# A layer loop in another order, two PSUM banks to an instruction, and the stores issued by ScalarE

## The reference, cut to what matters

```python
x_ft = jnp.fft.rfft2(v)
out1 = jnp.einsum('bixy,ioxy->boxy', x_ft[:, :, :M1, :M2], W1)
out2 = jnp.einsum('bixy,ioxy->boxy', x_ft[:, :, -M1:, :M2], W2)
...
x1 = jnp.fft.irfft2(out_ft, s=(Sx, Sy))
x2 = jnp.einsum('bcxy,cd->bdxy', v, w_w[i]) + w_b[i][None, :, None, None]
v = x1 + x2
mean = jnp.mean(v, axis=(0, 2, 3), keepdims=True)
var = jnp.var(v, axis=(0, 2, 3), keepdims=True)
v = (v - mean) * jax.lax.rsqrt(var + BN_EPS)
v = v * bn_g[i][None, :, None, None] + bn_b[i][None, :, None, None]
if i < L - 1:
    v = jax.nn.relu(v)
```

## Time and profile before

| | |
|---|---|
| median of 3 runs | 3470.16 us (3431.05 to 3483.62) |
| the profiled execution | 3436.51 us, its span 3434.7 us |
| busy share of the span: TensorE, VectorE, ScalarE, GpSimd | 82%, 62%, 45%, 18% |
| mean granted clock of TensorE | 0.896 of full |
| evictions L794 in the three loops | 768, the first at 222.1, the last at 2015.6 us |
| data moved | 541 MB, 158 GB/s over the span |

### The profile page before, as it was taken

How to read it: one execution, slowest core, us unless ns; L and a number is a source line. 1 busy time by engine, 2 the same in 40 slices (tenths; PEclk the granted TensorE clock), 3 DMA queues, 4 the chain that set the end, 5 groups by cost and what they waited for, 6 DMA issues and landing times. The chain is left out here.

```text
span 3434.7 us, 105530 instructions
## 1 busy us (share of the span) xinstructions
PE 2801.5 (82%) x45316; PEld 1467.6 (43%) x45316; DVE 2131.9 (62%) x3133; ACT 1547.3 (45%) x3432; POOL 605.7 (18%) x758
## 2 busy tenths in 40 slices
PE   0389999997899999789999985833478862999999
PEld 0145555554455555345555542211266650333333
DVE  2677777676577777567777753016467654455555
ACT  1255666564566666456666642001101110566665
POOL 0002333110033321003332110000144430000000
PEclk9889999898899999889999997976777766999999
DMA  5036666553888887478888863971122202567775
GB/s 161 11 86 161 149 140 142 123 140 101 246 256 255 250 251 241 126 195 259 256 255 251 255 194 142 405 230 37 46 63 67 66 20 58 96 119 120 119 121 90
DMA packets 244004, 541.34 MB, mean 158 GB/s; under 512 B 77857, under 2 KB 124705, under 8 KB 229953
## 3 DMA queue, kind: packets, MB, share of 16 engines
q1 hardware_dynamic: 234320, 529.04, 56.5%
q10 hardware_dynamic: 9264, 6.11, 0.9%
HBM read 320.28 MB, written 214.78 MB: 156 GB/s over the span
## 5 line engine op out<-in xcount | busy, mean ns | idle before, releaser
L794 ACT ACTIVATE p_v<-p_ps,k_scale_bias 128x512 f32<-128x512 f32 x768 | 536.8, 777 | 533.8 <-PE p_ps L900 533.8
L778 POOL COPY k_xm<-p_sp 64x288 f32<-64x288 f32 x384 | 264.6, 689 | 1566.2 <-DVE p_sp L301 1549.4
L801 ACT ACTIVATE p_ps<-p_ps 128x512 f32<-128x512 f32 x768 | 454.7, 593 | 116.6 <-PE p_ps L915 116.6
L900 PEld LDWEIGHTS p_ps<-k_idfty,p_t 64*128 64x128 f32 x6144 | 384.6, 199 | 184.9 <-issue 175.6
L296 DVE STREAM_TRANSPOSE p_at<-p_ps 128x1024 f32<-128x1024 f32 x192 | 228.5, 1228 | 358.5 <-PE p_ps L269 358.5
L291 DVE STREAM_TRANSPOSE p_vt<-p_v 128x1024 f32<-128x1024 f32 x384 | 448.4, 1211 | 3.0 <-ACT p_v L794 3.0
L900 PE MATMUL p_ps<-k_idfty,p_t 64*128 64x128 f32 x6144 | 423.3, 291 | 6.1 <-DVE p_t L663 4.1
L2034 DVE TENSOR_TENSOR x_ht<-x_ht,x_mask 128x384 f32<-128x384 f32 x512 | 268.3, 555 | 247.3 <-ACT x_ht L2008 246.5
L663 DVE STREAM_TRANSPOSE p_t<-p_ps 128x1024 f32<-128x1024 f32 x192 | 353.3, 1912 | 64.5 <-PE p_ps L656 64.0
L2008 ACT ACTIVATE x_ht<-x_ph,x_b 128x384 f32<-128x384 f32 x576 | 303.3, 578 | 195.5 <-PE x_ph L2055 195.5
L915 PE MATMUL p_ps<-p_v,k_wbd 32*32 32x512 f32 x6144 | 362.4, 605 | 6.3 <-ACT p_ps L801 4.6
(11 more groups left out here) (298 smaller groups left out, 3121.6 us busy)
## 6 DMA issues: line engine op xcount, KB each, us to landing
field<-p_v SPq DMA_DIRECT2D x768, 256.0 KB, 4.2
p_v<-field SPq DMA_DIRECT2D x64, 2048.0 KB
x_mask<-expert_weights SPq DMA_DIRECT2D x32, 1536.0 KB, 14.0
l_v<-field SPq DMA_DIRECT2D x16, 2048.0 KB, 25.9
k_xm<-field SPq DMA_DIRECT2D x12, 2048.0 KB, 24.8
k_mixw<-in_L_tok_fw_dram SPq DMA_DIRECT2D x16, 1152.0 KB, 10.5
at_cf<-state_coefficients SPq DMA_DIRECT2D x32, 384.0 KB
k_mixw<-field SPq DMA_DIRECT2D x4, 2048.0 KB, 23.8
```

What stands on the lines that cost most here:

```text
L778: nc.gpsimd.tensor_copy(view[64 * k:64 * k + 64, :, j, :, G * i:G * i + G], sp[64 * j:64 * j + 64, :, :, 16 * k:16 * k + M1].rearrange("p ...
L794: nc.scalar.activation(v[:, i % 3, at:at + CH], ps[:, e, g, :], ACT.Relu, bias=bias, scale=scale)\
L801: nc.scalar.activation(ps[:, e, a, :], ps[:, e, a, :], ACT.Square, accum_out=K["zs"][:, at:at + 1]).then_inc(s.sq_done, 1)
L900: ins = nc.tensor.matmul(ps[:, e, 2 * q + h, col:col + 128], lines, K["idfty"][rows, :], start=False, stop=True, skip_group_check=True)
```

## The change

The jobs stay the same. Four things are different:

- ScalarE's evictions and squares take two banks (1024 columns) in one instruction, and the counts of `uo_ready`, `sq_done`, `um_done` and `zq_done` are halved or set to pairs of banks; `zs` has half as many sums.
- The order of the jobs on TensorE, ScalarE and VectorE. TensorE: `channels(i-1, 1)`, `pixels(i, 1)`, `spectrum(i+1)`, `y_product(i-1)`, `pixels(i+1, 0)`, `x_product(i-1)`, `channels(i, 0)`. ScalarE: eviction of (i, 1), of (i+1, 0), then both squares of image i. VectorE: `pixels_turn(i-1, 1)`, `inverse_turn(i+1)`, `rows_turn(i-1)`, `pixels_turn(i, 0)`, `modes_turn(i-1)`, `spectrum_turn(i+2)`. The sets of banks that the jobs take change with it.
- The waits: in `pixels`, half 0 waits for the inverse turns ahead of L890 and not ahead of L900, half 1 for the squares of the image before; `channels(i, 0)` waits for the eviction of the next image's first half.
- The stores are issued by ScalarE, four DMAs behind the two evictions of a half, and no longer by SP. So ScalarE waits for its own eviction, issues, and goes on.

```diff
-            def store(i):
-                b = i % 3
-                for half in range(2):
-                    eng.wait_ge(s.uo_ready, NCH * i + G * half + G)
-                    for a in range(4):
-                        rows, cols = slice(C * a, C * a + C), slice(CH * half, CH * half + CH)
-                        eng.dma_start(V[i].rearrange("(g c) (a m) -> a c g m", g=G, a=4)[a][:, :, cols],
-                                      v[rows, b].rearrange("p (g m) -> p g m", g=G)[:, :, cols]).then_inc(u_out[b], 16)
...
             def evict(i, e, half):
-                for g in range(G):
-                    at = 1024 * g + CH * half
-                    act.wait_ge(s.um_done, NCH * i + G * half + g + 1)
-                    nc.scalar.activation(v[:, i % 3, at:at + CH], ps[:, e, g, :], ACT.Relu, bias=bias, scale=scale)\
-                        .then_inc(s.uo_ready, 1)
+                field = v[:, i % 3].rearrange("p (g m) -> p g m", g=G)
+                for q in range(2):
+                    act.wait_ge(s.um_done, 4 * i + 2 * half + q + 1)
+                    nc.scalar.activation(field[:, 2 * q:2 * q + 2, CH * half:CH * half + CH], ps[:, e, 2 * q:2 * q + 2, :], ACT.Relu,
+                                         bias=bias, scale=scale).then_inc(s.uo_ready, 1)
+
+            def store(i, half):
+                act.wait_ge(s.uo_ready, 4 * i + 2 * half + 2)
+                for a in range(4):
+                    rows, cols = slice(C * a, C * a + C), slice(CH * half, CH * half + CH)
+                    act.dma_start(V[i].rearrange("(g c) (a m) -> a c g m", g=G, a=4)[a][:, :, cols],
+                                  v[rows, i % 3].rearrange("p (g m) -> p g m", g=G)[:, :, cols]).then_inc(u_out[i % 3], 16)
...
+            evict(0, 0, 0)
+            store(0, 0)
             for i in range(n):
                 e = i % 2
-                evict(i, e, 0)
                 evict(i, e, 1)
+                store(i, 1)
+                if i + 1 < n:
+                    evict(i + 1, 1 - e, 0)
+                    store(i + 1, 0)
                 squares(i, 1 - e, 0)
-                squares(i, 1 - e, 1)
+                squares(i, e, 1)
...
-            inverse_turn(0, 1)
+            inverse_turn(0, 0)
+            spectrum_turn(1)
             for i in range(n):
                 e = i % 2
                 if i >= 1:
                     pixels_turn(i - 1, 1)
-                if i >= 2:
-                    modes_turn(i - 2, 1 - e)
                 if i + 1 < n:
-                    spectrum_turn(i + 1)
+                    inverse_turn(i + 1, 1 - e)
                 if i >= 1:
-                    rows_turn(i - 1, 1 - e)
+                    rows_turn(i - 1, e)
                 pixels_turn(i, 0)
-                if i + 1 < n:
-                    inverse_turn(i + 1, e)
+                if i >= 1:
+                    modes_turn(i - 1, e)
+                if i + 2 < n:
+                    spectrum_turn(i + 2)
...
                 for g in range(G):
-                    if half == 1:
-                        pe.wait_ge(s.uo_ready, NCH * i + g + 1)
-                    elif i >= 1:
-                        pe.wait_ge(s.sq_done, NCH * i - G + g + 1)
+                    if half == 0:
+                        pe.wait_ge(s.t_ready, 2 * i + g // 2 + 1)
+                    elif i == 0:
+                        pe.wait_ge(s.uo_ready, g // 2 + 1)
+                    else:
+                        pe.wait_ge(s.sq_done, 4 * (i - 1) + g // 2 + 1)
...
             for i in range(n):
                 e = i % 2
-                pixels(i, e, 0)
                 if i >= 1:
-                    y_product(i - 1, 1 - e)
+                    at_least(pe, s.sp_ready, i - 1)
+                    channels(i - 1, 1 - e, 1)
                 pixels(i, e, 1)
+                if i + 1 < n:
+                    spectrum(i + 1, 1 - e)
                 if i >= 1:
-                    pe.wait_ge(s.a2_ready, 2 * i)
-                else:
-                    pe.wait_ge(s.next_in, 64)
+                    pe.wait_ge(s.uo_ready, 4 * i + 4)
+                    y_product(i - 1, e)
+                if i + 1 < n:
+                    pixels(i + 1, 1 - e, 0)
+                if i >= 1:
+                    x_product(i - 1, e)
                 channels(i, 1 - e, 0)
```

More of the change, by code:

```diff
@@ L603, in norm_vector @@
     else:
-        c.then(ve.tensor_reduce(t[:, 1:2], K["zs"][:, 0:NCH * n], AX.X, ALU.add))
+        c.then(ve.tensor_reduce(t[:, 1:2], K["zs"][:, 0:4 * n], AX.X, ALU.add))
         c.then(ve.tensor_tensor(t[:, 0:1], t[:, 0:1], t[:, 1:2], ALU.add))
@@ L767, in _ @@
                     load(i + 2)
-                store(i)
             for b in range(3):
@@ L790, in evict @@
             def evict(i, e, half):
[L791 to L795 removed]
+                field = v[:, i % 3].rearrange("p (g m) -> p g m", g=G)
[9 more added lines that the diff above has]
+                                  v[rows, i % 3].rearrange("p (g m) -> p g m", g=G)[:, :, cols]).then_inc(u_out[i % 3], 16)
             def squares(i, e, half):
[L798 to L801, removed]
+                for q in range(2):
+                    act.wait_ge(s.zq_done, 4 * i + 2 * half + q + 1)
+                    at = 4 * i + 2 * half + q
+                    nc.scalar.activation(ps[:, e, 2 * q:2 * q + 2, :], ps[:, e, 2 * q:2 * q + 2, :], ACT.Square,
                                          accum_out=K["zs"][:, at:at + 1]).then_inc(s.sq_done, 1)
@@ L836, in pixels_turn @@
                 for pair in range(2):
-                    dve.wait_ge(s.uo_ready, NCH * i + G * half + 2 * pair + 2)
+                    dve.wait_ge(s.uo_ready, 4 * i + 2 * half + pair + 1)
                     at_least(dve, s.fy_done, i)
@@ L901, in pixels @@
                                                        start=False, stop=True, skip_group_check=True)
-                                if d == 1 and b1 == 1:
-                                    ins.then_inc(s.um_done, 1)
+                    ins.then_inc(s.um_done, 1)
             def channels(i, e, half):
-                if half == 1:
-                    pe.wait_ge(s.uo_ready, NCH * i + NCH)
                 for a in range(4):
                     if half == 1:
-                        pe.wait_ge(s.sq_done, NCH * i + a + 1)
+                        pe.wait_ge(s.uo_ready, 4 * i + 2 + a // 2 + 1)
+                    elif i + 1 < n:
+                        pe.wait_ge(s.uo_ready, 4 * (i + 1) + a // 2 + 1)
+                    else:
+                        pe.wait_ge(s.sq_done, 4 * (i - 1) + 2 + a // 2 + 1)
                     if a == 0:
@@ L921, in spectrum @@
                 for q in range(2):
-                    at_least(pe, s.uo_ready, NCH * i - G + 2 * q + 2 if i else 0)
+                    if i >= 2:
+                        pe.wait_ge(s.sq_done, 4 * (i - 2) + 2 + q + 1)
                     pe.nop(nofuse=True)
@@ L937, in _ @@
             mix_tensor(nc, pe, s, K, M, first)
+            pe.wait_ge(s.ms_done, 2 * NB)
             pe.wait_ge(s.zt_done, 2 * NB)
-            spectrum(0, 1)
-            norm_tensor(nc, pe, s, K, first, n_t, n_s, n_1, ps[:, 0, 0])
+            spectrum(0, 0)
+            norm_tensor(nc, pe, s, K, first, n_t, n_s, n_1, ps[:, 1, 0])
             if not first:
                 pe.wait_ge(s.w_in, 64)
+            pixels(0, 0, 0)
             pe.wait_ge(s.aggr, 2)
+            pe.wait_ge(s.next_in, 64)
             for i in range(n):
                 e = i % 2
-                pixels(i, e, 0)
                 if i >= 1:
-                    y_product(i - 1, 1 - e)
+                    at_least(pe, s.sp_ready, i - 1)
+                    channels(i - 1, 1 - e, 1)
                 pixels(i, e, 1)
+                if i + 1 < n:
+                    spectrum(i + 1, 1 - e)
                 if i >= 1:
-                    pe.wait_ge(s.a2_ready, 2 * i)
-                else:
-                    pe.wait_ge(s.next_in, 64)
-                channels(i, 1 - e, 0)
-                if i + 1 < n:
-                    spectrum(i + 1, e)
-                channels(i, 1 - e, 1)
-                if i >= 1:
-                    pe.wait_ge(s.t_ready, 2 * i + 4 if i + 1 < n else 2 * i + 2)
-                    x_product(i - 1, e)
-            y_product(n - 1, 1)
-            pe.wait_ge(s.sq_done, NCH * n)
+                    pe.wait_ge(s.uo_ready, 4 * i + 4)
[4 more added lines that the diff above has]
+                    x_product(i - 1, e)
+                channels(i, 1 - e, 0)
+            pe.wait_ge(s.sp_ready, n - 1)
+            channels(n - 1, 1, 1)
+            pe.wait_ge(s.sq_done, 4 * (n - 1) + 2)
+            y_product(n - 1, 0)
             x_product(n - 1, 0)
```

16 lines of the change are left out of this document (7 added, 9 removed).

## The result

| | before | after |
|---|---|---|
| median of 4 runs | 3456.28 us (3431.05 to 3483.62) | 3772.45 us (3757.41 to 3782.07) |
| ratio, 95% interval | | 1.0961 [1.092, 1.1003] |
| span of the profiled execution | 3434.7 us | 3771.0 us |
| mean granted clock of TensorE | 0.896 | 0.826 |

What follows compares the result with a forecast made beforehand. It took TensorE and ScalarE passing banks to and fro as the bound. Per layer 30 x 1.03 - 5 + 6.5 = 32.4 us, 97 for three layers, on 3470 gives 3567 us; range 3430 to 3740 (8 in 10).

Steps and rivals of the forecast that it cites:

- The chain: Steps done one after the other in an image across TensorE, VectorE and ScalarE: period 17.45 us against 16.42.
- Q0: ScalarE's first square of an image; forecast to start behind the end of the four store issues, not with L915's end.
- The store issue: Four store DMAs issued by ScalarE behind an eviction: hold it 2.9 us, range 1.7 to 3.3.
- Rival 1: Store issue is cheap on ScalarE, 1.7 us for four: period 16.25, 3455 us; chance 0.15.
- Rival 2: Stores hide altogether, issue running under the first channel block: period 15.6, 3395 us; chance 0.12.
- The clock: TensorE's falls to 1.2 GHz: excess of before left in the sum, nothing added; more falls made a rival.
- the excess of 22 us a layer: Second layer's 31 intervals before took 22 us more than 31 x 16.42, partly clock; left as it is.
- The last sign that the prediction named for being wrong: Granted clock in the three loops falling well below that of before.
- Rival 3: Lower clock takes a piece of most images: 2.1 us each, 3756 us in all; chance 0.18.
- the thin place of 3.5 us: TensorE between the second channel block's end (11.9) and the next L900 (15.45), 1.5 us of it idle.
- The tail: End of a layer, behind its last `pixels` half 0: some 6.5 us more than the old order's 24.1.
- What the order could bring: Period of an image in the new order without the store issue on its path: 15.6 us.

Runs made afterwards that it cites:

- e9: Changed kernel with the matmuls of only the second pair of banks of each second channel block run twice; 3590.28 us, 1.0454 to before.
- e11: Changed kernel with the first half's four store DMAs issued between the two squares instead of ahead of both; 3480.62 us, 1.0151 to before.
- e1: Changed kernel (new order, wide instructions) with the stores issued by SP again; 3431.44 us, 0.996 to before.
- e5: e1 with second- and third-layer loads, from the fourth on, bringing 256 of 4096 columns; 3365.14 us, 0.9716 to before.
- e7: e1 with the matmuls of the whole second channel block run twice; 3552.09 us, 1.0247 to before.

## Why the prediction was wrong, point by point

*The chain, right.* The period at full clock was forecast at 17.45 and is 17.47 in e9, with no step off by more than 0.12. The wide eviction takes 1.20, the pair 2.30, the wide square 1.01. No wait for a load stands in the profile, and Q0 started with the issue's end. E1 and St1 had their cover but for five images near the start of the layers, where St1 took 8.3 to 10.1 us and E0 waited for it.

*The store issue, right.* 2.9 was taken; 2.86 is measured. Rival 1 (1.7 for four) and Rival 2 (hidden under C0) fall with it. What the prediction said beside it, that an issuing engine is held for the whole time, is true of the instructions behind the issue alone, as e11 shows. The sentence of the Trainium skill, "DMA: Bandwidth & Descriptors", section "Issuing engines are not separate DMA queues", that the sequencer's time "is usually small relative to the DMA itself", speaks of one DMA. This trace doesn't contradict it: an issue takes 0.7 us (a quarter of 2.86), its DMA lands 4.0 us after it in the median. The prediction set four issues against it, and it was wrong that by this sentence the move would be harmless. Small beside the DMA isn't free: on the chain the four count in full.

*The clock: the step that failed.* "I leave the excess of 22 us a layer as it is in the sum, for the falls depend on how the period lies to them." That put the added price of the clock at nothing. But the falls didn't depend on luck. The lengthened wait for Q0 is in every image, so in 90 of 93 intervals the clock falls, and its price is on the chain each time: 20.47 - 17.47 = 3.0 us, some 280 us over 93 intervals. The kernel before exceeded 93 intervals of 16.42 by 71 us. The prediction kept that excess; in the changed kernel it doesn't come on top of the 280, so the net is 209. With 98 for the chain (1.05 an interval), -14 for the intervals that are not 20.47, the first of each layer above all, and 44 outside the 93 intervals, that makes the 336. Forecast were 0, 93, -15 and 19.5. The last sign that the prediction named for being wrong, a granted clock well below that of before, came true.

Rival 3 had the mechanism and the place ("the thin place of 3.5 us"), with 0.18 and a price of 2.1. That its 3756 came near 3772 is in part luck: its price was too small, and it kept the old excess on top. Its argument against, that the clock stood at 1.00 over 1000 to 1160 with waits of the same sort, compared unlike things: before, banks came back one by one, and L915 and L890 spread their matmuls over the wait, where now TensorE does nothing for 1.77 us. In the first layer part of the falls is the order's own, as e1 shows.

*Its price, mis-sized.* Between 1072.78 and 1077.66, L903 takes 3.71 to the next block, not 1.98, and S to I 1.17, not 0.95. L894's two pairs, from Q0's start to L903, take 4.09, not 3.21; Rival 3 left this term of 0.88 out, scaled L900 by another line's ratio (1.4 for 1.73), and gave S too much. That is 2.8 for this image of 20.2 us.

The section "HAM oscillation — how this bites in real kernels" of "TensorE: Matmul & The Clock Gate" in the Trainium skill says that a wait which lets the clock fall is paid again in each tile of the loop and not once. This trace agrees: the clock falls in 90 of the 93 intervals, in the median 20.5 us after the last time.

*The tail, somewhat short.* 6.5 us more were forecast behind a layer's last P0; the last copies start 10.7 us later than before, 34.8 against 24.1, and a passage is 14 us longer. The first interval of the second and third layer is 12.8, where 12.3 was forecast.

*What the order could bring*, 15.6 us an image, is real (15.7 in e5) but was never at hand: the full loads take 1.0 us an image back in the mean (519.1 us for 31 intervals in e1, 488.3 in e5), and in the first layer the clock takes more. The stops that the trace shows are about half of that, 17 us of the second layer against 4; the other half is in longer rows of matmuls and isn't explained.

## What to carry to other kernels

A DMA issue on a compute engine is an instruction on its chain: place it where nobody waits for what comes behind it, or where it runs under compute that is ahead of it and that it needn't wait for. Here the same eight issues cost 10% of the time with four of them ahead of the squares, 1.5% with these four between the squares, and nothing with all eight behind the other eviction. When a change lengthens a wait of TensorE that recurs in each iteration, price it twice, by itself and with the lower clock over all the matmuls that follow it, L894's groups too, and take the second for likely when the granted clock already falls now and then. Filler in a gap is a cheap test of that: if more work makes a kernel faster and the granted clock rises with it, the gap let the clock fall. Try it with less filler too, since a whole block can become the bound itself (e7).

## What the runs showed of the hardware

- The fall and the loop lock together. In all three layers the median interval is 20.45 to 20.48 us, the clock falls in 90 of 93 of them and stays down for 6.8 us (median), though TensorE is busy 90% of each layer (567 of 630 us).
- With 16 matmul instructions more an image (0.55 us), in a gap of 1.77 us, the clock stayed up in 51 of the 62 intervals of the second and third layer, and in 6 of 31 of the first.
- TensorE stops inside blocks for 0.4 to 3.1 us under full DMA traffic, with no semaphore involved, 27 times in two layers of e1; with a sixteenth of the load in those layers (151 GB/s instead of 252) 5 times. 25 of the 27 end 1.3 to 1.6 us after a packet of the instruction queue.
- The issue of four DMAs of 256 KB takes 2.86 us in the median on ScalarE and on SP alike. The four are unequal: 0.31, 0.45, 0.70 and 1.30 us in the median for St0 on ScalarE.
- Five times, at the second or third image of a layer, St1's four issues held ScalarE for 8.3 to 10.1 us. Each of the five ended within 0.7 us of the landing of a weight load (L327, 1152 KB) that SP had issued before; no run leaves the weight load out.
- Issues on ScalarE run at the same time as the compute instructions ahead of them (e11: four issues in 2.86 us, of which Q1 waits 0.93).
